# Smaller token tiles in the first mixture-of-experts layer of a two-layer perceiver kernel

## The chip, the cores and the metric

The kernel is one program on one core of a Trainium2 chip. The metric is the device time of one execution in microseconds (us). TensorE (PE) multiplies, VectorE (DVE), ScalarE (ACT) and GpSimd (POOL) do the element-wise work, and SyncE (SP) issues most of the transfers, which all run on the core's 16 DMA engines.

## The reference, cut to what matters

Two layers transform 512 tokens of 512 numbers. Each has a cross attention over 8192 context rows, a sequence mixer and a mixture of experts. The change concerns the experts of the first layer:

```
capacity = int(512 / 8 * 1.25) + 1            # 81
top1 = argmax(softmax(x @ wg));  rank = place of the token among those of its expert
valid = rank < capacity                        # tokens beyond the 81st get nothing
buf[expert * capacity + rank] = x              # 8 experts x 81 rows x 512
h = gelu(buf @ W1 + b1)                        # 512 -> 2048
y = h @ W2 + b2                                # 2048 -> 512
out = where(valid, y[slot], 0) * combine_w;  x = x + out
```

In the second layer each token goes to two of eight experts without a limit.

## The kernel before

The stages run one after the other, with a barrier between them: `ProjectContext` (keys and values of both layers from the context, 32 chunks of 512 rows), `CrossAttention`, `SelectiveScan`, `Experts` (layer 0), then attention, `DeltaRule` and `Experts` (layer 1). The same class does both expert layers; `self.two` is true in layer 1.

**Experts of layer 0.** A tile is the rows of one expert, so there are 8 tiles (`self.tiles`). Rows travel through two scratch tensors in HBM, `x_slots` and `y_slots`, in which tile `j` has the 128 rows `j * P` to `(j + 1) * P`. A token has row `e * 128 + rank`, or a spare row in tiles 8 to 11 if it is beyond capacity. Only rows 0 to 80 of a tile can be named by a token. POOL scatters the normalized rows into `x_slots` (L1562), and at the end gathers from `y_slots` (L1568). Tile 0 takes no such way in: `select_x` (L1581) builds it by a matmul with a 0/1 matrix. The last tile takes no such way out: its result is spread by a matmul (L1650).

**Weights.** Each tile needs 8 pieces of 1 MB of weights (4 of W1, 4 of W2), `moe_raw`, six buffers (`RAW`). Every fp32 operand is cut into a high and a low fp32r part: ACT makes the high part (L1656), DVE the low part (L1660), both of 128 x 2048 elements, three pieces ahead of PE (`AHEAD`), into four buffers (`CUT`). `product` (L93) then makes three matmuls of each pair. In all of them the token rows are the stationary operand and the 512 columns of the weights are the moving one, so a piece is 12 matmuls of 512 columns. For each of four blocks of 512 hidden numbers, `leave_hidden` copies the result (L1680), PE turns it (`turn_hidden`, four transposes, L1609), ACT applies gelu with the bias (L1691, four instructions of 128 x 128), and DVE makes the high and low parts (L1744, L1746). After the second W2 piece of a tile PE turns the next tile's rows (`turn_x`, L1588), and ACT and DVE cut them (L1671, L1728). DVE adds the output bias (L1783) and raises `y_done`.

**Order of the transfers.** SP works through one list in order (`loads_and_stores`, L1519). A piece `g` waits for the low part of piece `g - 6`. Ahead of pieces 6 and 7 of tile `j` stands the store of tile `j - 1`, which waits for its `y_done`; behind piece 0 of tile `j` stand the load of its rows and the load of its output bias (256 KB). So at each `y_done` SP sends, back to back, the store of the finished tile, pieces 6 and 7 of the tile that begins, piece 0 of the one after it, that tile's rows and bias, and then pieces 1 to 5 as buffers come free.

**Zeros.** In iteration 2 of `ProjectContext` SP stores zeros over all of `x_slots` (15 stores of 256 KB, L201) and over six tiles of `y_slots` (L203). The other tiles of `y_slots` get all their rows from the experts. Behind them in SP's list stand the store of the chunk's values (L226) and, in the next iteration, four stores of 512 KB of cut context (L172), on which `split_chunk` of ACT (L285) waits two iterations later (`parts_out`), and a store of the queries (L731).

Of the kernel before, what the change touches and what calls it, by code (L numbers as in the profile page):

```python
# [5 lines left out]
F32 = mybir.dt.float32  # L6
# [20 lines left out]
CAPACITY = int(TOK / EXPERTS * 1.25) + 1  # L27
FT = FF // P
# [71 lines left out]
class ProjectContext:  # L100
# [62 lines left out]
    def loads_and_stores(self, sp):  # L163
# [29 lines left out]
        for m in range(self.CHUNKS):  # L193
# [4 lines left out]
            if m == self.STORE_ZEROS:  # L198
                sp.wait_ge(*self.zeroed.at(1))
                for t in range(TILES1):  # L200
                    sp.dma_start(S["x_slots"][t * P:(t + 1) * P, :], self.nothing[:]).then_inc(*self.zeros_out.up())  # L201
                for tile in (EXPERTS - 1, *range(EXPERTS, EXPERTS + TT), TILES1 - 1):
                    sp.dma_start(S["y_slots"][tile * P:(tile + 1) * P, :], self.nothing[:]).then_inc(*self.zeros_out.up())  # L203
# [1086 lines left out]
class Experts:  # L1290
# [11 lines left out]
    def __init__(self, c, A, S, x, l, out=None):  # L1302
# [4 lines left out]
        self.choices = 2 if self.two else 1  # L1307

    def run(self):
        c, l = self.c, self.l  # L1310
        with ExitStack() as st:
# [22 lines left out]
            self.xg = c.sb(st, n + "xg", [P, 2, 2, KD, P], F32R)  # L1334
            self.h = c.sb(st, n + "h", [P, FF])
            self.ht = c.sb(st, n + "ht", [P, 2, FT, P], F32R)
            self.yrow = c.sb(st, n + "yrow", [P, 2, D])
            if not self.two:
                self.bias1 = c.sb(st, n + "bias1", [P, EXPERTS, FT])
                self.bias2 = c.sb(st, n + "bias2", [P, 2, D])  # L1340
                self.act_out = c.sb(st, n + "act_out", [P, 2, self.JB, P])
# [177 lines left out]
    def loads_and_stores(self, sp):  # L1519
        n, xs, ys = f"moe{self.l}_w", self.S["x_slots"], self.S["y_slots"]  # L1520

        def store(j):
            sp.wait_ge(*self.y_done.at(j + 1))
            sp.dma_start(ys[j * P:(j + 1) * P, :], self.yrow[:, j % 2, :]).then_inc(*self.y_out[j % 2].up())
# [3 lines left out]
        for j in range(self.tiles):  # L1528
# [3 lines left out]
            for w in range(self.pieces):  # L1532
# [4 lines left out]
                if w == (5 if j == 0 else 0):  # L1537
# [4 lines left out]
                    if j:  # L1542
                        sp.dma_start(self.xrow[:, j % 2, :], xs[j * P:(j + 1) * P, :]).then_inc(*self.xrow_in[j % 2].up())
# [30 lines left out]
    def on_pe(self, pe):  # L1574
        c, bank, ht, cut, JB = self.c, self.c.bank, self.ht, self.cut, self.JB

        def select_x():
            pe.wait_ge(*self.selected.at(TT))
            for k in range(KD):
                for t in range(TT):  # L1580
                    last = pe.matmul(bank[self.X_BANK][:, k * P:(k + 1) * P], self.norm.rows[:, t, k * P:(k + 1) * P], self.select[:, t, :], start=t == 0, stop=t == TT - 1)  # L1581
            last.then_inc(*self.x_turned.up())

        def turn_x(j):
            pe.wait_ge(*self.xrow_in[j % 2].at((j + 1) // 2))
            pe.wait_ge(*self.xg_low.at(j))
            for k in range(KD):
                last = pe.transpose(bank[self.X_BANK][:, k * P:(k + 1) * P], self.xrow[:, j % 2, k * P:(k + 1) * P], c.ident[:])  # L1588
# [8 lines left out]
        def out_of_hidden(g, db):  # L1597
            pe.wait_ge(*self.low.at(g + 1))
            for i in range(JB):
                f = db * JB + i  # L1600
                last = product(pe, bank[self.OUT_BANK], [ht[:, part, f, :] for part in range(2)], [cut[:, g % self.CUT, part, i, :] for part in range(2)], f == 0, f == FT - 1)
            last.then_inc(*self.used.up())

        def turn_hidden(j, fb):
# [3 lines left out]
            for i in range(JB):  # L1608
                last = pe.transpose(bank[self.TURN_BANK + fb % 2][:, i * P:(i + 1) * P], self.h[:, (fb * JB + i) * P:(fb * JB + i + 1) * P], c.ident[:])  # L1609
            last.then_inc(*self.h_turned.up())  # L1610

        def tile(j):
# [7 lines left out]
            for fb in range(FB):  # L1620
# [5 lines left out]
                else:  # L1626
                    into_hidden(j, g + fb, bank[fb])
# [21 lines left out]
        for t in range(TT):  # L1649
            pe.matmul(bank[t], self.spread_t[:, t, :], self.yrow[:, (self.tiles - 1) % 2, :], start=True, stop=True).then_inc(*self.last_made.up())  # L1650
# [11 lines left out]
    def on_act(self, act):  # L1662
        bank, JB, last_piece = self.c.bank, self.JB, self.tiles * self.pieces
# [5 lines left out]
        def x_high(j):  # L1669
            act.wait_ge(*self.x_turned.at(j + 1))  # L1670
            act.copy(self.xg[:, j % 2, 0], bank[self.X_BANK].rearrange("p (k n) -> p k n", k=KD)).then_inc(*self.xg_high.up())  # L1671

        def leave_hidden(j, fb):
# [4 lines left out]
            else:  # L1678
                act.wait_ge(*self.used.at(j * self.pieces + fb + 1))
                act.copy(part, bank[fb]).then_inc(*self.h_done.up())  # L1680

        def leave_turned(j, fb):
# [7 lines left out]
            for i in range(JB):  # L1690
                act.activation(self.act_out[:, fb % 2, i, :], b[:, i * P:(i + 1) * P], ACT.Gelu, bias=self.bias1[:, j, fb * JB + i:fb * JB + i + 1]).then_inc(*self.gelu.up())  # L1691
# [27 lines left out]
    def on_dve(self, dve):  # L1719
        bank, JB, last_piece = self.c.bank, self.JB, self.tiles * self.pieces  # L1720
# [5 lines left out]
        def x_low(j):  # L1726
            dve.wait_ge(*self.xg_high.at(j + 1))
            dve.tensor_tensor(self.xg[:, j % 2, 1], bank[self.X_BANK].rearrange("p (k n) -> p k n", k=KD), self.xg[:, j % 2, 0].bitcast(F32), ALU.subtract).then_inc(*self.xg_low.up())  # L1728
# [31 lines left out]
        for j in range(self.tiles):  # L1760
# [15 lines left out]
            if not self.two:  # L1776
# [6 lines left out]
                dve.tensor_tensor(self.yrow[:, j % 2, :], bank[self.OUT_BANK], self.bias2[:, j % 2, :], ALU.add).then_inc(*self.y_done.up())  # L1783
# [597 lines left out]
```

## Time and profile before

| | |
|---|---|
| Time, median of 3 runs | 3687.98 us (3680.82 to 3688.92) |
| Span of the profiled execution | 3690.2 us (no other time is given for it) |
| PE, DVE, ACT, POOL busy | 97%, 70%, 54%, 48% of the span |
| First expert layer | from about 1705 to 1932 us of the span |
| Mean DMA rate | 170 GB/s |

The span runs from the first to the last instruction. Busy time of an engine is a share of that; PE's is counted from modelled ends of pipelined matmuls, so 97% doesn't mean that 97% is work at full speed. The question for each stage is which engine, or which transfer, sets its pace.

### The profile page before, as it was taken

Reading aid. Unit: us, or ns where it says so; the run is one execution under the profiler, and the core shown is the slowest. Engines: PE = TensorE matmul, PEld = TensorE weight load, DVE = VectorE, ACT = ScalarE, POOL = GpSimd, SP = SyncE. Lnnn points to the kernel's source line nnn. Section 1 sums busy time; section 2 is a strip of 40 time slices with the busy share of each in tenths; the row PEclk is TensorE's granted clock in tenths of the full one; section 3 lists DMA queues with packets and bytes.
Section 4 is the critical chain, followed back from the end, with each engine's and each line's share of the span. In section 5 each row is a group of like instructions: output and inputs, shape, how many; then the busy total and the mean of one; then the engine's idle time right before and its main releaser. Section 6 shows DMA issues by size and latency. Waiting matters only on the chain. (4 is left out here: it accounts for less than half of the span.)

```text
span 3690.2 us, 46629 instructions
## 1 busy us (share of the span) xinstructions
PE 3575.8 (97%) x17916; PEld 2313.7 (63%) x17916; DVE 2570.7 (70%) x3497; ACT 1981.7 (54%) x2320; POOL 1781.2 (48%) x744
## 2 busy tenths in 40 slices
PE   8999999999999999988999999999999897999999
PEld 6788788654554555446876545555554476788887
DVE  3222344587787787557996877877876465899998
ACT  2122322466666666634973666666666421777776
POOL 2122222489889989700001889989988320100001
PEclk9999999999999999998998999999999998999999
DMA  7777776532332332046978433333331100999998
GB/s 274 252 246 228 244 236 202 178 92 69 91 92 71 88 92 73 18 173 224 362 296 237 108 91 72 89 92 77 83 92 31 52 1 20 366 376 368 379 377 302
DMA packets 249723, 628.46 MB, mean 170 GB/s; under 512 B 43632, under 2 KB 137872, under 8 KB 194976
## 3 DMA queue, kind: packets, MB, share of 16 engines
q1 hardware_dynamic: 210720, 552.08, 46.2%
q10 hardware_dynamic: 36864, 67.13, 4.9%
q0 software_dynamic: 1920, 6.29, 0.5%
q8 instruction: 143, 2.34, 0.3%
q14 instruction: 76, 0.62, 0.1%
HBM read 488.46 MB, written 136.87 MB: 169 GB/s over the span
## 5 line engine op out<-in xcount | busy, mean ns | idle before, releaser
L790 DVE TENSOR_REDUCE maxima<-psum 128x1 f32<-128x512 f32 x2048 | 1286.1, 683 | 344.2 <-PE psum L785 341.6
L961 POOL TENSOR_TENSOR exp_sums<-pt 128x1024 f32<-128x1024 f32 x342 | 816.8, 2389 | 296.0 <-PE psum L834 147.1
L785 PE MATMUL psum<-ks,first_q 96*128 96x512 f32 x2048 | 805.4, 434 | 4.8 <-DMA ks<-k_parts 0.6
L949 ACT ACTIVATE pt<-psum 128x1024 f32<-128x1024 f32 x704 | 717.6, 1026 | 142.7 <-PE psum L814 116.2
L964 POOL TENSOR_TENSOR exp_sums<-exp_sums,pt 128x1024 f32<-128x1024 f32 x310 | 737.4, 2379 | 44.4
L830 PE MATMUL psum<-pt,vs 128*32 128x512 f32 x4096 | 675.6, 600 | 7.1 <-issue 2.3
L785 PEld LDWEIGHTS psum<-ks,first_q 96*128 96x128 f32 x2048 | 386.9, 189 | 455.2 <-DVE maxima L790 318.1
L834 PE MATMUL psum<-exp_sums,constants 128*32 128x512 f32 x1408 | 671.4, 600 | 0.0
L814 PE MATMUL psum<-qs,ks 97*128 97x512 f32 x2048 | 656.2, 404 | 3.1 <-PEq L87 3.1
L1660 DVE TENSOR_TENSOR moe_cut<-moe_raw,moe_cut 128x2048 fp32r<-128x2048 f32 x244 | 556.9, 2290 | 55.9 <-ACT moe_cut L1656 48.6
L1656 ACT CAST moe_cut<-moe_raw 128x2048 fp32r<-128x2048 f32 x244 | 468.9, 1923 | 55.5 <-PE psum L97 47.0
L944 ACT ACTIVATE pt<-psum 128x512 f32<-128x512 f32 x320 | 191.2, 597 | 482.4 <-PE psum L814 480.1
L814 PEld LDWEIGHTS psum<-qs,ks 97*128 97x128 f32 x2048 | 389.5, 191 | 96.0 <-ACT pt L949 18.2
L372 POOL TENSOR_TENSOR cparts<-cx,cparts 128x2048 fp32r<-128x2048 f32 x32 | 147.8, 4620 | 521.5 <-ACT cparts L285 521.5
L830 PEld LDWEIGHTS psum<-pt,vs 128*32 128x32 f32 x4096 | 139.9, 109 | 342.4 <-issue 240.5
L1568 POOL DMA_INDIRECT ln_m_rows<-y_slots,row_of x8 | 13.2, 1653 | 667.2 <-DMA y_slots<-moe_yrow 665.4
L354 DVE SCALAR_TENSOR_TENSOR kparts<-psum,bk,kparts 128x512 fp32r<-128x512 f32 x128 | 96.1, 751 | 274.4 <-ACT kparts L311 274.4
L95 PE MATMUL psum<-moe_cut,moe_xg 128*128 128x512 f32 x608 | 241.6, 397 | 3.3 <-DVE moe_xg L1728 3.3
L97 PE MATMUL psum<-moe_cut,moe_xg 128*128 128x512 f32 x608 | 237.4, 390 | 0.0
L96 PE MATMUL psum<-moe_cut,moe_xg 128*128 128x512 f32 x608 | 236.6, 389 | 0.0
L95 PE MATMUL psum<-cparts,wk_high 128*128 128x512 f32 x512 | 205.7, 402 | 19.8 <-POOL cparts L372 16.8
L311 ACT ACTIVATE kparts<-psum,bk 128x512 fp32r<-128x512 f32 x128 | 88.1, 688 | 245.1 <-PE psum L97 227.3
(337 smaller groups left out, 4835.3 us busy)
## 6 DMA issues: line engine op xcount, KB each, us to landing
moe_raw<-in_moe_w SPq DMA_DIRECT2D x244, 1024.0 KB, 8.3
ks<-k_parts SPq DMA_DIRECT2D x384, 256.0 KB, 4.6
k_parts<-kparts ACTq DMA_DIRECT2D x256, 256.0 KB, 4.2
cx<-in_ctx SPq DMA_DIRECT2D x32, 1024.0 KB, 6.2
vs<-v_heads SPq DMA_DIRECT2D x32, 1024.0 KB, 5.3
v_heads<-vrow SPq DMA_DIRECT2D x25, 1024.0 KB, 5.1
late_context<-cparts SPq DMA_DIRECT2D x28, 512.0 KB, 11.7
late_parts<-late_context SPq DMA_DIRECT2D x28, 512.0 KB, 4.6
```

The source lines that it names most:

```text
L95: pe.matmul(out, lhs[0], rhs[0], start=start, stop=False)
L97: return pe.matmul(out, lhs[1], rhs[0], start=False, stop=stop)
L785: pe.matmul(self.c.bank[self.FIRST_BANK + k % 3], self.first_q[s][:, t * P:(t + 1) * P], self.ks[s][part][0:3 * DH, at:at + CHUNK], start= ...
L790: dve.tensor_reduce(self.maxima[:, h % 2, i % TT, i // TT:i // TT + 1], self.c.bank[self.FIRST_BANK + k % 3], X, ALU.max).then_inc(*self.f ...
L814: last = pe.matmul(bank[self.SECOND_BANK + 2 * (pair % 2) + j], ks[h % 2][part][:, at:at + P], qs[h % 2][:], start=True, stop=True)
L830: last = pe.matmul(bank[self.OUT_BANK][g * DH:(g + 1) * DH, :], vs[h % 2][:, tiles[i], :], pt[:, slot + i, :], start=b == 0 and r == 0, st ...
L834: last = pe.matmul(bank[self.OUT_BANK][3 * DH:4 * DH, :], c.ones[:, 0:DH], item, start=b == 0 and r == 0, stop=b == NB - 1 and r == min(se ...
L949: act.activation(self.pt[:, to:to + 2, :], self.c.psum[:, at:at + 2, :], ACT.Exp).then_inc(*self.exp.up())
L961: engine.tensor_tensor(to, self.pt[:, slot:slot + R, :], self.pt[:, slot + R:slot + 2 * R, :], ALU.add).then_inc(*signal.up())
L964: engine.tensor_tensor(to, to, self.pt[:, slot + (n + 1) * R:slot + (n + 2) * R, :], ALU.add).then_inc(*signal.up())
L1656: act.copy(self.cut[:, g % self.CUT, 0], self.raw[:, g % self.RAW]).then_inc(*self.high.up())
L1660: dve.tensor_tensor(self.cut[:, g % self.CUT, 1], self.raw[:, g % self.RAW], self.cut[:, g % self.CUT, 0].bitcast(F32), ALU.subtract).then ...
```

## The change

`ROWS0` is 82: the capacity of 81, made even. A tile of layer 0 is held in 82 rows in place of 128 (`self.held`); layer 1 keeps 128. In layer 0 this changes:

- the stationary operands have 82 columns, the moving ones still 512, and outputs lie in 82 partitions;
- the transposes take 82 rows and an 82 x 82 identity, `select_x` moves 82 columns;
- ACT and DVE instructions on `xg`, `ht` and `act_out` handle 328 or 82 columns in place of 512 or 128, those on `h` and `yrow` 82 partitions and still 512 columns;
- the load of a tile's rows and the store of a tile's result cover 82 rows of 2 KB (168 KB) in place of 128 (256 KB). The tile's place in HBM stays 128 rows apart. The bias load stays at 128 rows;
- `ProjectContext` gets seven more stores of zeros, over rows 82 to 127 of tiles 0 to 6 of `y_slots` (46 rows, 94 KB each), because no expert writes these any longer. They stand between the 15 stores to `x_slots` and the six to `y_slots`.

The cutting of the weights, the number of matmuls and the order of SP's list in the expert stage don't change.

```diff
+ROWS0 = CAPACITY + CAPACITY % 2
...
                 for t in range(TILES1):
                     sp.dma_start(S["x_slots"][t * P:(t + 1) * P, :], self.nothing[:]).then_inc(*self.zeros_out.up())
+                for tile in range(EXPERTS - 1):
+                    sp.dma_start(S["y_slots"][tile * P + ROWS0:(tile + 1) * P, :], self.nothing[ROWS0:P, :]).then_inc(*self.zeros_out.up())
                 for tile in (EXPERTS - 1, *range(EXPERTS, EXPERTS + TT), TILES1 - 1):
...
+        self.held = P if self.two else ROWS0
...
-            self.xg = c.sb(st, n + "xg", [P, 2, 2, KD, P], F32R)
+            self.xg = c.sb(st, n + "xg", [P, 2, 2, KD, self.held], F32R)
...
-            self.ht = c.sb(st, n + "ht", [P, 2, FT, P], F32R)
+            self.ht = c.sb(st, n + "ht", [P, 2, FT, self.held], F32R)
...
-                self.act_out = c.sb(st, n + "act_out", [P, 2, self.JB, P])
+                self.act_out = c.sb(st, n + "act_out", [P, 2, self.JB, self.held])
...
-            sp.dma_start(ys[j * P:(j + 1) * P, :], self.yrow[:, j % 2, :]).then_inc(*self.y_out[j % 2].up())
+            sp.dma_start(ys[j * P:j * P + self.held, :], self.yrow[0:self.held, j % 2, :]).then_inc(*self.y_out[j % 2].up())
...
-                        sp.dma_start(self.xrow[:, j % 2, :], xs[j * P:(j + 1) * P, :]).then_inc(*self.xrow_in[j % 2].up())
+                        sp.dma_start(self.xrow[0:self.held, j % 2, :], xs[j * P:j * P + self.held, :]).then_inc(*self.xrow_in[j % 2].up())
...
-                    last = pe.matmul(bank[self.X_BANK][:, k * P:(k + 1) * P], self.norm.rows[:, t, k * P:(k + 1) * P], self.select[:, t, :], start=t == 0, stop=t == TT - 1)
+                    last = pe.matmul(bank[self.X_BANK][:, k * P:k * P + R], self.norm.rows[:, t, k * P:(k + 1) * P], self.select[:, t, 0:R], start=t == 0, stop=t == TT - 1)
...
-                last = pe.transpose(bank[self.X_BANK][:, k * P:(k + 1) * P], self.xrow[:, j % 2, k * P:(k + 1) * P], c.ident[:])
+                last = pe.transpose(bank[self.X_BANK][:, k * P:k * P + R], self.xrow[0:R, j % 2, k * P:(k + 1) * P], c.ident[0:R, 0:R])
...
-                last = product(pe, bank[self.OUT_BANK], [ht[:, part, f, :] for part in range(2)], [cut[:, g % self.CUT, part, i, :] for part in range(2)], f == 0, f == FT - 1)
+                last = product(pe, bank[self.OUT_BANK][0:R, :], [ht[:, part, f, :] for part in range(2)], [cut[:, g % self.CUT, part, i, :] for part in range(2)], f == 0, f == FT - 1)
...
-                last = pe.transpose(bank[self.TURN_BANK + fb % 2][:, i * P:(i + 1) * P], self.h[:, (fb * JB + i) * P:(fb * JB + i + 1) * P], c.ident[:])
+                last = pe.transpose(bank[self.TURN_BANK + fb % 2][:, i * P:i * P + R], self.h[0:R, (fb * JB + i) * P:(fb * JB + i + 1) * P], c.ident[0:R, 0:R])
...
-                    into_hidden(j, g + fb, bank[fb])
+                    into_hidden(j, g + fb, bank[fb][0:R, :])
...
-            act.copy(self.xg[:, j % 2, 0], bank[self.X_BANK].rearrange("p (k n) -> p k n", k=KD)).then_inc(*self.xg_high.up())
+            act.copy(self.xg[:, j % 2, 0], bank[self.X_BANK].rearrange("p (k n) -> p k n", k=KD)[:, :, 0:R]).then_inc(*self.xg_high.up())
...
-                act.activation(self.act_out[:, fb % 2, i, :], b[:, i * P:(i + 1) * P], ACT.Gelu, bias=self.bias1[:, j, fb * JB + i:fb * JB + i + 1]).then_inc(*self.gelu.up())
+                act.activation(self.act_out[:, fb % 2, i, :], b[:, i * P:i * P + R], ACT.Gelu, bias=self.bias1[:, j, fb * JB + i:fb * JB + i + 1]).then_inc(*self.gelu.up())
...
-                dve.tensor_tensor(self.yrow[:, j % 2, :], bank[self.OUT_BANK], self.bias2[:, j % 2, :], ALU.add).then_inc(*self.y_done.up())
+                dve.tensor_tensor(self.yrow[0:R, j % 2, :], bank[self.OUT_BANK][0:R, :], self.bias2[0:R, j % 2, :], ALU.add).then_inc(*self.y_done.up())
```

The copy out of the hidden banks (L1680), the low part of the rows (L1728) and the spreading matmul of the last tile (L1650) are cut to `R` in the same way.

## Rows read from the trace of the kernel before

**Rows 1.** Busy time by stretch, all engines (stretch, us, engines, PEclk, DMA share, GB/s).

```profile
core 0: us, PE busy (x) PEld busy (x) DVE busy (x) ACT busy (x) POOL busy (x), PEclk, DMA share, GB/s
1761.00:1905.00 144.00, 144.00 (x696) 119.13 (x695) 140.12 (x114) 128.90 (x175) 0.00 (x0) 1.00 0.95 383
1767.00:1783.00 16.00, 16.00 (x80) 13.25 (x79) 15.90 (x14) 14.16 (x19) 0.00 (x0) 1.00 1.01 418
1784.00:1786.00 2.00, 2.00 (x11) 1.65 (x10) 2.00 (x3) 1.72 (x2) 0.00 (x0) 1.00 0.25 102
1725.10:1731.10 6.00, 5.85 (x32) 5.66 (x32) 4.63 (x17) 0.23 (x2) 2.08 (x1) 0.64 0.60 247
...
80.00:110.00 30.00, 30.00 (x119) 21.81 (x117) 8.90 (x13) 5.35 (x6) 4.52 (x1) 1.00 1.06 373
110.00:120.00 10.00, 10.00 (x44) 7.88 (x43) 3.85 (x6) 0.97 (x1) 0.00 (x0) 1.00 0.39 122
```

**Rows 2.** Groups by line and shape, 1704 to 1932 us (busy, mean ns, idle before).

```profile
L1660 DVE TENSOR_TENSOR moe_cut<-moe_raw,moe_cut 128x2048 fp32r<-128x2048 f32 x64 | 145.6, 2287 | 12.5 <-ACT moe_cut L1656 12.5
L1656 ACT CAST moe_cut<-moe_raw 128x2048 fp32r<-128x2048 f32 x64 | 124.2, 1944 | 8.4 <-PE psum L97 5.1 <-DMA moe_raw<-in_moe_w 3.2
...
L1691 ACT ACTIVATE moe_act_out<-psum,moe_bias 128x128 f32<-128x128 f32 x128 | 37.8, 408 | 0.0
...
L1609 PE MATMUL psum<-constants,moe_h 128*128 128x128 f32 x128 | 19.1, 272 | 0.0
```

**Rows 3.** Chain of waits, 1761 to 1905 us: who waited for whom, total, times, longest.

```profile
ACT moe_cut L1656 <- DMA moe_raw<-in_moe_w: 2.3, 3, 1.1
```

**Rows 4.** SP's queue in order of time (start, us, line, transfer, count).

```profile
1761.00 0.33 SPq L1524 DMA_DIRECT2D y_slots<-moe_yrow  x1
1761.37 1.41 SPq L1536 DMA_DIRECT2D moe_raw<-in_moe_w  x3
1762.82 0.60 SPq L1543 DMA_DIRECT2D moe_xrow<-x_slots  x1
...
1904.88 0.33 SPq L1524 DMA_DIRECT2D y_slots<-moe_yrow  x1
1905.25 0.92 SPq L1536 DMA_DIRECT2D moe_raw<-in_moe_w  x2
```

**Rows 5.** Store of a tile's result, 1704 to 1935 us: issue to landing.

```profile
DMA to landing us min/median/max: 2.1/2.2/3.1
```

**Rows 6.** PE in order of time about a group of transposes.

```profile
1810.70 0.39 PE L97 MATMUL psum<-moe_cut,moe_xg 128*128 128x512 f32 x1
...
1810.93 0.60 PE L1609 MATMUL psum<-constants,moe_h 128*128 128x128 f32 x4
...
1811.28 0.48 PE L95 MATMUL psum<-moe_cut,moe_xg 128*128 128x512 f32 x1
...
1811.60 0.40 PE L96 MATMUL psum<-moe_cut,moe_xg 128*128 128x512 f32 x1
```

**Rows 7.** End of the stage: the gathers (ns, first and last start), landing, and DVE.

```profile
L1568 POOL DMA_INDIRECT ln_m_rows<-y_slots,row_of x4: 949/1472/2186, 1907.3 to 1912.1; - x4
...
DMA to landing us min/median/max: 4.1/4.6/6.3
...
1921.09 2.73 DVE L1755 SCALAR_TENSOR_TENSOR x_rows<-ln_m_rows,small,x_rows 128x512 f32<-128x512 f32 x4
1925.92 0.69 DVE L1783 TENSOR_TENSOR moe_yrow<-psum,moe_bias 128x512 f32<-128x512 f32 x1 [2.10 <-PE psum L97]
```

**Rows 8.** About the stores of zeros: SP, ACT and DVE in order of time.

```profile
72.57 14.93 SPq L201 DMA_DIRECT2D x_slots<-nothing  x15
...
92.47 0.64 SPq L226 DMA_DIRECT2D v_heads<-vrow  x1
...
119.03 1.91 ACT L285 CAST cparts<-cx 128x2048 fp32r<-128x2048 f32 x1 [13.86 <-PE psum L97]
...
133.41 0.43 DVE L724 CAST qparts<-qf 128x512 fp32r<-128x512 f32 x1 [3.36 <-DMA q_parts<-qparts]
```

More of the change, by code:

```diff
@@ L1574, in on_pe @@
     def on_pe(self, pe):
-        c, bank, ht, cut, JB = self.c, self.c.bank, self.ht, self.cut, self.JB
+        c, bank, ht, cut, JB, R = self.c, self.c.bank, self.ht, self.cut, self.JB, self.held
         def select_x():
@@ L1649, in on_pe @@
         for t in range(TT):
-            pe.matmul(bank[t], self.spread_t[:, t, :], self.yrow[:, (self.tiles - 1) % 2, :], start=True, stop=True).then_inc(*self.last_made.up())
+            pe.matmul(bank[t], self.spread_t[0:R, t, :], self.yrow[0:R, (self.tiles - 1) % 2, :], start=True, stop=True).then_inc(*self.last_made.up())
     def high_part(self, act, g):
@@ L1662, in on_act @@
     def on_act(self, act):
-        bank, JB, last_piece = self.c.bank, self.JB, self.tiles * self.pieces
+        bank, JB, R, last_piece = self.c.bank, self.JB, self.held, self.tiles * self.pieces
         def high(g):
@@ L1679, in leave_hidden @@
                 act.wait_ge(*self.used.at(j * self.pieces + fb + 1))
-                act.copy(part, bank[fb]).then_inc(*self.h_done.up())
+                act.copy(part[0:R, :], bank[fb][0:R, :]).then_inc(*self.h_done.up())
         def leave_turned(j, fb):
@@ L1719, in on_dve @@
     def on_dve(self, dve):
-        bank, JB, last_piece = self.c.bank, self.JB, self.tiles * self.pieces
+        bank, JB, R, last_piece = self.c.bank, self.JB, self.held, self.tiles * self.pieces
         def low(g):
@@ L1727, in x_low @@
             dve.wait_ge(*self.xg_high.at(j + 1))
-            dve.tensor_tensor(self.xg[:, j % 2, 1], bank[self.X_BANK].rearrange("p (k n) -> p k n", k=KD), self.xg[:, j % 2, 0].bitcast(F32), ALU.subtract).then_inc(*self.xg_low.up())
+            dve.tensor_tensor(self.xg[:, j % 2, 1], bank[self.X_BANK].rearrange("p (k n) -> p k n", k=KD)[:, :, 0:R], self.xg[:, j % 2, 0].bitcast(F32), ALU.subtract).then_inc(*self.xg_low.up())
         def leave_hidden(j, fb):
```

## The prediction

> **What bounds the kernel now.** I read the busy time by stretch first, to find what sets the pace of the stage that changes. From 1761 to 1905 us, six tiles of the first expert layer, PE has no gap: 144.00 of 144.00 us, at the full granted clock [rows 1]. Between the first and the last store of a tile's result lie 143.88 us for six tiles, so a tile takes 23.98 us [rows 4]. DVE is busy 140.12 us of the 144, ACT 128.90, and the DMA engines 95%, so three others stand close behind PE. The groups by line say what they do: DVE's time is mostly the 64 low parts of the weights at 2287 ns, ACT's the 64 high parts at 1944 ns [rows 2]; neither depends on how many rows a tile has. The waits show that transfers are late three times, 2.3 us in all [rows 3], and those waits are ACT's, not PE's. So PE's stream is the bound, and behind it the transfers have little left: in a stretch with a full queue they run at 418 GB/s with a share of 1.01 [rows 1], which is 26.1 GB/s for each of 16 engines.
>
> **What the change does to PE.** The 96 matmuls of a tile move 512 columns as before, so they cost what they cost. What shrinks is the moving operand of 20 transposes a tile. Between the L97 before a group of four and the second matmul after it lie 0.90 us [rows 6]; an ordinary step takes 0.23 us, as from that L97 to the first transpose, and two of them lie in it, so four transposes cost 0.44 us, 0.11 us each. Bounds for one with 82 columns: nothing saved (if the load of its 128 columns of weights sets the step), or 46/128 of it, 0.04 us. That is 0 to 0.8 us a tile, 0 to 6 us for eight. `select_x`, 32 records in 5.85 us, lies on the path at the start, mostly at the low clock (0.64 [rows 1]); it gives 0 to 2.1 us by the same ratio. The first cut of the rows on ACT and DVE gives some 0.3 us. If nothing else moves, the change is worth 0 to 8 us; I would take 4.
>
> **ACT and DVE.** Gelu on 82 columns in place of 128 is shorter than 408 ns, and L1744 and L1746 handle 328 columns in place of 512. At most 46/128 of 16 x 0.41 us on ACT goes, 2.4 us a tile, and DVE loses at most 46/128 of its small work (about 23.35 us a tile less 8 x 2.29, so 5.1), 1.8 us. Both lie beside PE's stream. Their worth is nothing as long as PE has no gap.
>
> **The transfers.** A tile's rows and its result shrink from 262 KB to 168 KB each. Spread over all 16 engines that lowers the load of an engine from 573 to 562 KB a tile (8 pieces of 65.5 KB, the bias 16.4, and 2 x 10.5 in place of 2 x 16.4). But nothing in this trace shows a transfer of 82 rows of 2 KB, and 82 rows can't be dealt out evenly over 16: 128 is 16 x 8, 82 is 2 x 41. The two ends are 16 engines (5 or 6 rows each) and 2 engines (41 rows each); 128-row transfers run near 16 x 26.1 GB/s [rows 1], which fits equal shares and says nothing of 82. I take 2 engines: an equal deal is the simplest rule by which hardware could cut a copy without a remainder, and 2 is the largest number up to 16 that divides 82.
>
> The Trainium skill says so outright ("DMA: Bandwidth & Descriptors", section "Why a DMA increments its semaphore by 16 and not by 1"): a copy issued from SP uses the largest number of engines up to 16 that divides the slowest dimension of both sides, always the lowest-numbered ones. By it both 82-row and 46-row copies run on the same 2 engines; no row here tests it.
>
> **Price of 2 engines in the expert stage.** Each of the two engines then carries 8 x 65.5 + 16.4 + 2 x 84.0 = 708 KB a tile. At 26.1 GB/s that is 27.1 us, more than PE's 23.98. A weight piece has landed only when its slowest engine is done, so from then on the tile takes 27.1 us. The slack ahead of PE takes up part. I therefore count the queue of these two engines through to the end, from the first store of a result, at 1761.00 [rows 4]. SP has been standing there, and the queue runs empty while it does, as the share of 0.25 just about the next store, at 1784 to 1786 us, shows [rows 1]. In front of the last piece stand 50 pieces (14 to 63), 7 stores of results, 6 loads of rows, 6 of the bias: 3275 + 588 + 504 + 98 = 4465 KB, 171.1 us. A store of 256 KB into an empty queue lands 2.2 us after its issue [rows 5], of which 0.6 us is moving 16.4 KB per engine, so 1.6 us is fixed. The last piece lands at 1761.0 + 1.6 + 171.1 = 1933.7. Behind it come ACT 1.94, DVE 2.29 [rows 2] and 12 matmuls at 0.23, 2.8 us: PE is done at 1940.7, against 1925.9 before (start of L1783 [rows 7]): **+14.8 us**. The queue stays full in between: at each `y_done` SP hands it a store, three pieces, the next rows and the bias, and then five pieces as buffers come free, 27.1 us of work for a tile.
>
> What is late next is the gather. It starts when the store of tile 6 has landed, before at 1907.3; now that store has pieces 62 and 63 behind it, 5.0 us, so it lands at 1928.7. The last of four gathers is issued 4.8 us later and lands at most 6.3 us after that [rows 7], 1939.8; DVE's last add-back of 0.7 us ends at 1940.5. That is just when PE ends, so I add 0.3. Stage: **+15 us**. PE's 0 to 8 us are not seen then, since the transfers set the end.
>
> **Price in the first stage.** The seven new stores of zeros (46 rows, 94 KB) have the same problem: 46 is 2 x 23. They give two engines 47 KB each seven times, 330 KB, 12.6 us. Spread evenly they would be 659 KB, 1.6 us. They stand behind the 15 stores to `x_slots`, which SP issues at 1.0 us each, the pace of full queues [rows 8]. From 80 to 110 us the DMA share is 1.06, and in the next 10 us 0.39 [rows 1], so only about 6 us of those 12.6 find free room. Late then are the store of values (92.47), the four stores of cut context, on which ACT's cut at 119.03 depends, and the store of queries, on which DVE already waited 3.36 us at 133.41 [rows 8]. Bounds: 0 (ACT's K work and PE have slack of several us) and 12.6 (all passed on). I take 4, since the last of those waits has no slack.
>
> **Sum.** 15 + 4 = +19 us: the profiled execution, whose span of 3690.2 is the only time given for it and lies 2.2 above the median, would show 3709; on the median of 3688, **3707 us**.
>
> **The rivals.**
>
> *Even spreading.* If an 82-row copy uses all 16 engines, the load per engine falls, the zeros are hidden, and PE's savings are all that is left: 3688 - 4 = 3684, range 3680 to 3688. This is the case that ends faster, or unchanged. The mechanism decides by the number of engines: with n of them a loaded engine carries 541 + 336/n KB, and 23.98 us at 26.1 GB/s is 626 KB, so with 4 or more PE remains the bound. For it speaks only that nothing in the trace contradicts it. Chance 0.12.
>
> *Two engines, but absorbed.* The weights are issued up to six pieces ahead, 6 x 2.5 = 15 us. If the queue's lead over PE at 1761 covers more than my count, or an engine alone runs faster than 26.1 GB/s when the other 14 rest, the stage loses under 5 us: 3688 to 3694. Against it: the count runs to the last piece, and the lead is in it, since the last piece is now issued at 1906 and used only at 1923 or so. The rate would have to rise to 28.5 GB/s to take the 14.8 away. Chance 0.07.
>
> *Two engines, and slower than counted.* Copies of 2 KB rows cost an engine more than pieces of 8 KB a partition, and rows and results both are of that kind. At 20 GB/s for those 13 transfers (84 KB, 4.2 us in place of 3.2) the stage loses 13 us more, and the zeros up to 8 more: 3721 to 3728. The 15 stores of zeros, of the same rows, fill the engines at 373 GB/s for 80 to 110 us [rows 1], 0.9 of the rate I used, so a little of this is likely. Chance 0.11.
>
> *Forecast as summed*: 0.70, its own range 3697 to 3720.
>
> **How the numbers follow.** The likeliest case gives 3707. Eight in ten: below 3689 lies the even spreading, 0.11 or so, above 3725 the worst of the slower case, 0.07; hence 3689 to 3725. A change of this kernel can be told from none at about 0.2%, 7.4 us. Faster by more: half of the even case at best, 0.04. Within: the rest of that case and most of the absorbed one, with a little of the forecast's low end, 0.13. Slower: 0.83.
>
> **What the changed profile would show.** The store of a result should land 5 us or more after its issue where it took 2.2, even into an empty queue (3.2 us of moving in place of 0.6). The distance from one such store to the next should grow from 23.98 to about 27 us, with PE idle before L1588 and L95, and ACT's L1656 waiting for `moe_raw`. The DMA share of 1761 to 1905 should fall below 0.95 though the stage is bound by transfers, as 14 engines rest. SP should be stuck for some 12 us more at the stores of zeros, and PE should show gaps, or a late start, between 105 and 140 us. The gelu of 82 columns should be under 408 ns and change nothing. The prediction is wrong if the result's store still lands in 2.2 us: then the copy is spread, and the time is PE's.

## The result

The changed kernel takes 3725.95 us (median of 4 runs, 3724.44 to 3727.28), the kernel before, on the same chip, 3686.81 (4 runs, 3680.82 to 3688.92): a ratio of 1.0106, 95% interval 1.0091 to 1.012. The change costs 39 us. The forecast was 3707, with 3725 as the upper end of its range: right in direction, and some 19 us too small. The profiled execution has a span of 3725.3 us, 35.1 more than before's 3690.2.

The lines of `Scratch` and of the expert stage stand four lines lower in the new file: before's L1524, L1543, L1568, L1588, L1656, L1660, L1691 and L1783 are L1528, L1547, L1572, L1592, L1660, L1664, L1695 and L1787 here.

**SP's queue** of the changed kernel, in order of time (start, us, line, transfer, count), first about the zeros and then in the expert stage:

```profile
93.26 12.29 SPq L206 DMA_DIRECT2D y_slots<-nothing  x6
105.60 1.13 SPq L229 DMA_DIRECT2D v_heads<-vrow  x1
...
1712.56 0.35 SPq L1362 DMA_DIRECT2D wr<-in_moe_router  x1
...
1769.26 0.26 SPq L1528 DMA_DIRECT2D y_slots<-moe_yrow  x1
...
1857.38 0.26 SPq L1528 DMA_DIRECT2D y_slots<-moe_yrow  x1
...
1886.30 0.26 SPq L1528 DMA_DIRECT2D y_slots<-moe_yrow  x1
...
1948.11 0.26 SPq L1528 DMA_DIRECT2D y_slots<-moe_yrow  x1
...
1976.35 0.33 SPq L679 DMA_DIRECT2D wq<-in_wq  x1
```

L1528 is the store of a tile's result, as L1524 was [rows 4]. From the first to the last there are now 1948.11 - 1769.26 = 178.85 us for six tiles, **29.81 us a tile** where it was 23.98 and the forecast said 27.1. The next stage's first load stands at 1976.35; before it stood at 1933.52. From the router's load at the top (1712.56; before 1705.21) the expert stage takes 263.8 us in place of 228.3, which is 35.5 more. And the stage begins 7.35 us later, most of which comes from the zeros: SP is stuck for 12.29 us in six of them, and the store of values that stood at 92.47 [rows 8] now stands at 105.60.

**Busy time by stretch** of the changed kernel (columns as in [rows 1]):

```profile
1769.26:1948.11 178.85, 153.58 (x697) 99.66 (x696) 134.58 (x114) 125.14 (x174) 0.00 (x0) 0.92 0.80 302
1873.00:1876.00 3.00, 0.29 (x3) 0.16 (x3) 2.97 (x4) 0.75 (x1) 0.00 (x0) 1.00 0.99 314
1876.00:1880.00 4.00, 4.00 (x14) 2.54 (x14) 0.88 (x2) 1.51 (x2) 0.00 (x0) 0.57 1.03 424
1824.00:1826.00 2.00, 2.00 (x11) 1.26 (x10) 1.79 (x2) 1.41 (x2) 0.00 (x0) 1.00 0.13 53
```

PE had no gap in these six tiles [rows 1]; now it is busy 153.58 of 178.85 us. The last line shows why. From 1824 to 1826 us ACT is still working through pieces as they land, yet the DMA share is 0.13 and 53 GB/s move. Two of 16 engines are 0.125, and twice 26.1 GB/s are 52. So 14 engines have nothing to do, while two carry the tail of every weight piece. The packets of the transfers say the same of all six tiles: exactly two engines are at work in 5.5 us of a tile, and one or none in 0.3 us. So the two loaded engines hardly ever rest. The share of the whole stretch fell from 0.95 to 0.80 in a stage that is now bound by its transfers.

**The chain of waits** of the changed kernel, 1769 to 1948 us (who waited for whom: total, times, longest):

```profile
DVE moe_cut L1664 <- ACT moe_cut L1660: 35.8, 29, 3.5
ACT moe_cut L1660 <- DMA moe_raw<-in_moe_w: 25.7, 22, 2.4
...
PE psum L1592 <- DMA moe_xrow<-x_slots: 20.3, 5, 5.3
...
PE psum L1592 <- issue: 4.6, 1, 4.6
```

ACT waited 2.3 us in all for weight pieces [rows 3]; now it waits 25.7. PE itself waits 20.3 us in five waits at L1592, the transposes of the next tile's rows, the first of the two places that the forecast gave it. A sixth wait of 4.6 us, for which the profile names no releaser, stands at the same line. Together these are 24.9 of PE's 25.3 idle us. At the second place, the first matmul of a product, it never waits: the pieces come late for ACT, but still in time for PE, and what stops PE is the load of the next rows, which stands in the same queue behind the store and three pieces. One of the six, **PE in order of time**:

```profile
1872.74 0.40 PE L98 MATMUL psum<-moe_cut,moe_ht 128*82 128x512 f32 x1
1875.84 0.51 PE L1592 MATMUL psum<-constants,moe_xrow 82*128 82x82 f32 x4 [2.71 <-DMA moe_xrow<-x_slots]
1876.14 0.44 PE L96 MATMUL psum<-moe_cut,moe_ht 128*82 128x512 f32 x1
1876.42 0.48 PE L97 MATMUL psum<-moe_cut,moe_ht 128*82 128x512 f32 x1
1876.69 0.63 PE L98 MATMUL psum<-moe_cut,moe_ht 128*82 128x512 f32 x1
1877.12 0.63 PE L96 MATMUL psum<-moe_cut,moe_ht 128*82 128x512 f32 x1
```

Behind a wait of 2.71 us the steps between matmuls are 0.43 us in place of 0.23, and the granted clock of 1876 to 1880 is 0.57, mostly the lower level of 1.2 GHz. That makes PE slow for some 3 us just after it stood idle. It costs little here, since the two loaded engines stay at work meanwhile and set the pace.

**The store of a result.** The profile gives no landing for the stores of 82 rows, but their packets can be followed. The last of the 82 ends 5.4 to 7.0 us after the issue, 5.5 in the median; of the 128 before, 1.7 to 2.6 us, 1.7 in the median. In the store of 1797.88 all 82 packets take 84 ns, and they fill 3.41 us: that is 41 of them one behind the other, on each of two engines. The gather behind the last store, in the changed kernel:

```profile
L1572 POOL DMA_INDIRECT ln_m_rows<-y_slots,row_of x4: 950/1438/2561, 1954.2 to 1958.9; - x4
```

The first gather waits for the last store and comes 6.1 us after its issue (1948.11), where before it came 2.4 us after [rows 4, 7]. Even so it starts 14.6 us and the last one 9.9 us before the addition of the last product's bias (L1787), which starts at 1968.8 and waits for PE alone, 1.5 us. So the gather is not late.

### The profile page after: what moved, and what is told of

Same layout as the page of the kernel before. It is cut to its first block and busy times, and to the rows that moved or that the text cites. A ratio compares the mean times of both kernels' runs of the same rounds, so it can differ in the third digit from the quotient of the medians.

```text
span 3725.3 us, 46636 instructions
## 1 busy us (share of the span) xinstructions
PE 3578.3 (96%) x17916; PEld 2282.1 (61%) x17916; DVE 2561.5 (69%) x3497; ACT 1976.1 (53%) x2320; POOL 1781.2 (48%) x744
## 5 line engine op out<-in xcount | busy, mean ns | idle before, releaser
L1664 DVE TENSOR_TENSOR moe_cut<-moe_raw,moe_cut 128x2048 fp32r<-128x2048 f32 x244 | 557.6, 2291 | 93.0 <-ACT moe_cut L1660 87.0
L1660 ACT CAST moe_cut<-moe_raw 128x2048 fp32r<-128x2048 f32 x244 | 467.3, 1916 | 79.5 <-PE psum L98 44.8
L1572 POOL DMA_INDIRECT ln_m_rows<-y_slots,row_of x8 | 14.1, 1766 | 708.1 <-DMA y_slots<-moe_yrow 706.3
L96 PE MATMUL psum<-moe_cut,moe_xg 128*128 128x512 f32 (+1 forms) x608 | 241.9, 398 | 3.2 <-DVE moe_xg L1732 3.2
L98 PE MATMUL psum<-moe_cut,moe_xg 128*128 128x512 f32 (+1 forms) x608 | 238.0, 391 | 0.0
L97 PE MATMUL psum<-moe_cut,moe_xg 128*128 128x512 f32 (+1 forms) x608 | 237.5, 391 | 0.0
```

Source lines behind the costliest of these rows:

```text
L96: pe.matmul(out, lhs[0], rhs[0], start=start, stop=False)
L98: return pe.matmul(out, lhs[1], rhs[0], start=False, stop=stop)
L1660: act.copy(self.cut[:, g % self.CUT, 0], self.raw[:, g % self.RAW]).then_inc(*self.high.up())
L1664: dve.tensor_tensor(self.cut[:, g % self.CUT, 1], self.raw[:, g % self.RAW], self.cut[:, g % self.CUT, 0].bitcast(F32), ALU.subtract).then ...
```

## The experiments

Ten kernels, in an order that narrows the question: is it the number of rows in a copy, what do the zeros cost, which copy costs what, how does it go with the number of engines, and can the 82 rows be kept at no cost. "Tile" below is the distance between the first and the last store of a result, by six; "stage" runs from the router's load to the next stage's first load. Each ratio is against the kernel before on the same chip. The products and transposes have 84, 96 and 92 columns in e1, e2 and e8, 128 in e4_zeros46, and 82 in the others.

| kernel | rows in the stage's copies | tile, us | stage, us | median, us | before, us | ratio (95%) |
|---|---|---|---|---|---|---|
| before | 128 | 23.98 | 228.3 | | | |
| after | 82 | 29.81 | 263.8 | 3725.95 | 3686.81 | 1.0106 (1.0091 to 1.012) |
| e1_rows84 | 84 | 23.49 | 226.1 | 3680.45 | 3687.08 | 0.9981 (0.9972 to 0.999) |
| e2_rows96 | 96 | 23.75 | 225.8 | 3680.39 | 3687.08 | 0.9982 (0.9973 to 0.9991) |
| e3_dma128 | 128, products 82 | 23.46 | 225.8 | 3681.29 | 3687.08 | 0.9985 (0.9976 to 0.9994) |
| e4_zeros46 | before, with the zeros | 23.98 | 228.3 | 3693.42 | 3687.08 | 1.0019 (1.001 to 1.0029) |
| e5_zeros48 | 82, zeros 48 | 29.76 | 263.4 | 3717.14 | 3687.02 | 1.0084 (1.0071 to 1.0098) |
| e6_x82 | load 82, store 128 | 26.51 | 242.7 | 3698.88 | 3687.02 | 1.004 (1.0026 to 1.0054) |
| e7_y82 | load 128, store 82 | 24.97 | 236.2 | 3690.15 | 3687.02 | 1.001 (1.0001 to 1.0019) |
| e8_rows92 | 92 | 26.27 | 242.6 | 3696.75 | 3687.02 | 1.0028 (1.0017 to 1.0039) |
| e9_bias82 | bias 82, the rest 128 | 26.69 | 242.8 | 3698.49 | 3685.83 | 1.003 (1.0018 to 1.0042) |
| e10_split82 | 80 + 2, zeros 48 | 23.46 | 226.1 | 3681.13 | 3685.83 | 0.9985 (0.9976 to 0.9994) |

### The number of rows in a copy: e1, e2, e3

e1_rows84 against the changed kernel (84 is 14 x 6; the zeros are then 44 rows, 11 x 4):

```diff
-ROWS0 = CAPACITY + CAPACITY % 2
+ROWS0 = 84
```

> The changed kernel with 84 rows to a tile in place of 82: two rows more in every load, store, matmul and copy. Two-engine theory (a copy is dealt out in equal parts, over the largest number of engines up to 16 that divides its rows): 84 is 14 x 6 and the zeros' 44 rows are 11 x 4, so no engine gets much more than the others; the tile is back at PE's pace of 24.0 us or a little below, the first stage at its old length, the time 3680 to 3690 us. Rival (any copy of fewer than 128 rows is slow, or 82-column operands are): 84 is no better than 82, about 3725 us, a tile takes about 30 us.

e2_rows96 (96 is 16 x 6; the zeros are then 32 rows):

```diff
-ROWS0 = CAPACITY + CAPACITY % 2
+ROWS0 = 96
```

> The changed kernel with 96 rows to a tile: 96 is 16 x 6 and the 32 rows of zeros 16 x 2. Two-engine theory: all 16 engines share each copy, tile at PE's pace, 3680 to 3690 us, the same as with 84 rows within a microsecond or two. Rival (fewer rows are slow in themselves): between the kernels before and after, 3700 to 3715 us.

e3_dma128 computes with 82 rows, but copies 128 in both directions and stores no zeros; POOL clears `yrow` once in their place:

```diff
-                for tile in range(EXPERTS - 1):
-                    sp.dma_start(S["y_slots"][tile * P + ROWS0:(tile + 1) * P, :], self.nothing[ROWS0:P, :])...
...
-            sp.dma_start(ys[j * P:j * P + self.held, :], self.yrow[0:self.held, j % 2, :])...
+            sp.dma_start(ys[j * P:(j + 1) * P, :], self.yrow[:, j % 2, :])...
...
-                        sp.dma_start(self.xrow[0:self.held, j % 2, :], xs[j * P:j * P + self.held, :])...
+                        sp.dma_start(self.xrow[:, j % 2, :], xs[j * P:(j + 1) * P, :])...
...
+            pool.memset(self.yrow[:], 0.0).then_inc(*self.cleared.up())
...
+                if j == 0:
+                    dve.wait_ge(*self.cleared.at(1))
```

> The changed kernel with the two transfers of a tile back at 128 rows and without the seven stores of zeros; all of PE, ACT and DVE works on 82 rows as in the changed kernel. If the transfers are the whole loss, the time is at or below that of before, and the tile shows what the smaller compute is worth: 23.2 to 24.0 us for 23.98, 3679 to 3688 us. If the 82-row compute has a part in the loss, a tile stays above 24.5 us.

Two rows more take the whole loss away and turn it into a gain: 3680.45 where 82 rows gave 3725.95. e1, e2 and e3 agree within 1 us, though their copies hold 84, 96 and 128 rows. The first and the last store of a result in e1_rows84 (the row of the `moe_yrow` tile: ns min/median/max, first and last start):

```profile
L1528 SPq DMA_DIRECT2D y_slots<-moe_yrow x7: 340/340/341, 1757.6 to 1898.5; - x7
```

140.9 us for six tiles, against 178.85 with 82 rows. So the cause is how a copy of 82 rows is dealt out, and not its bytes, the shapes of the products or the zeros as such. This is also what the rule that the prediction cites (the Trainium skill, "DMA: Bandwidth & Descriptors", section "Why a DMA increments its semaphore by 16 and not by 1") makes of these sizes: 14 engines for 84 rows, 16 for 96 and 128, 2 for 82. The trace agrees with the 2 (share 0.13 at 53 GB/s), the times with the rest. A rival rule, the largest power of two that divides the rows, would put 84 rows on 4 engines, as it does the 92 of e8 below; but e8 has a tile of 26.27 us and e1 one of 23.49.

In e3_dma128 PE again has no gap, and the four transposes can be read (PE in order of time):

```profile
1811.55 0.39 PE L98 MATMUL psum<-moe_cut,moe_xg 128*82 128x512 f32 x1
1811.78 0.45 PE L1613 MATMUL psum<-constants,moe_h 82*128 82x82 f32 x4
1812.02 0.44 PE L96 MATMUL psum<-moe_cut,moe_xg 128*82 128x512 f32 x1
1812.30 0.40 PE L97 MATMUL psum<-moe_cut,moe_xg 128*82 128x512 f32 x1
```

From the L98 before them to the second matmul behind them 0.75 us, where it was 0.90 [rows 6]: with two steps of 0.23 in it, four transposes cost 0.29 us, 0.07 each, for 0.11. Twenty of them should save 0.75 us a tile; the tile fell by 0.52 (23.98 to 23.46). The median step between the other matmuls went from 0.227 to 0.230 us, which over 96 of them takes some 0.3 back.

### The zeros: e4, e5

e4_zeros46 is the kernel before with the seven stores of zeros and nothing else of the change:

```diff
+                for tile in range(EXPERTS - 1):
+                    sp.dma_start(S["y_slots"][tile * P + 82:(tile + 1) * P, :], self.nothing[82:P, :])...
```

> The kernel before with nothing but the seven stores of 46 rows of zeros added. Two-engine theory: the first stage is some 7 us longer as in the changed kernel, and the rest is unchanged, 3692 to 3697 us. Rival (the zeros are hidden and the later start of the expert stage has another cause): 3685 to 3689 us.

e5_zeros48 is the changed kernel with zeros over rows 80 to 127 (48 is 16 x 3; the results overwrite rows 80 and 81 later):

```diff
-                    sp.dma_start(S["y_slots"][tile * P + ROWS0:(tile + 1) * P, :], self.nothing[ROWS0:P, :])...
+                    sp.dma_start(S["y_slots"][tile * P + 80:(tile + 1) * P, :], self.nothing[80:P, :])...
```

> The changed kernel (82 rows) with the seven stores of zeros over rows 80 to 127, 48 rows, 16 x 3, in place of 46. Two-engine theory: the first stage is back at its old length, the expert stage keeps its whole loss: about 7 us less than the changed kernel, 3717 to 3721 us, a tile still 29.8 us. Rival (the late start also costs the expert stage, or the 2 engines don't explain the zeros): no change, 3724 to 3728 us.

e4 costs 0.19%, 0.10 to 0.29%, 6 to 7 us. e5 gives 8.8 us back of the changed kernel's 39.1, across two chips (3717.14 for 3725.95), and the expert stage is as slow as ever (29.76 us a tile), so the two losses are separate; 6.3 and 30.1 us, each against its own kernel before, add up to 39.1 within the intervals. SP in e4_zeros46, in order of time:

```profile
92.54 11.96 SPq L205 DMA_DIRECT2D y_slots<-nothing  x6
104.55 1.28 SPq L228 DMA_DIRECT2D v_heads<-vrow  x1
...
1710.51 0.34 SPq L1360 DMA_DIRECT2D wr<-in_moe_router  x1
```

The 12 us at the zeros are the 12.6 that the prediction counted for two engines. What they hold up is seen in the changed kernel's chain of waits, 90 to 140 us:

```profile
DVE vrow L369 <- DMA v_heads<-vrow: 9.8, 1, 9.8
...
PE psum L96 <- DVE vrow L369: 4.6, 1, 4.6
```

The store of values is 13 us late, DVE waits 9.8 us before it can write `vrow` again, and PE 4.6 us for DVE, its only wait from 90 to 140 us. Right behind that wait PE has no gap, but the granted clock is at its lower level (busy time by stretch of the changed kernel):

```profile
118.00:122.00 4.00, 4.00 (x10) 3.13 (x11) 2.29 (x4) 0.00 (x0) 0.00 (x0) 0.50 1.04 315
```

There the matmuls start every 0.43 us in place of 0.23, nine times, which adds some 1.8 us. Together that is 6.4, and SP's stores of values show it later on; kernel before, changed kernel and e4:

```profile
193.68 0.38 SPq L226 DMA_DIRECT2D v_heads<-vrow  x1
...
200.52 0.39 SPq L229 DMA_DIRECT2D v_heads<-vrow  x1
...
199.42 0.39 SPq L228 DMA_DIRECT2D v_heads<-vrow  x1
```

Less what already lay between the kernels ahead of the zeros (0.12 us more, and 0.70 less, at the store of 66.24), the zeros cost 6.7 us in the changed kernel and 6.4 in e4. The start of the expert stage, 7.35 and 5.3 us later, is a poorer measure: in the kernels without the 46-row zeros it lies anywhere from 1700.7 to 1705.8, before included.

### Which copy: e6, e7

Both ask whether the load of rows and the store of the result cost the same. e6_x82 is e3_dma128 with the load back at 82 rows:

```diff
-                        sp.dma_start(self.xrow[:, j % 2, :], xs[j * P:(j + 1) * P, :])...
+                        sp.dma_start(self.xrow[0:self.held, j % 2, :], xs[j * P:j * P + self.held, :])...
```

> As e3 (all transfers of 128 rows, no extra zeros), but the load of a tile's rows covers 82. Load of the two engines by my 26.1 GB/s: 8 x 65.5 + 16.4 + 16.4 + 84 = 641 KB, 24.6 us a tile, so hardly over PE's 23.5: 3682 to 3686 us. If a 2 KB row costs such an engine more than at full rate (about 0.12 us in place of 0.08, as the tile of 29.8 us in the changed kernel asks): 20.2 + 0.7 + 1.3 + 4.9, 26.5 to 27 us a tile, 3695 to 3705 us. PE also waits ahead of the turning of the rows (L1592).

e7_y82 is the changed kernel with the load at 128 rows and the zeros at 48, so that only the store has 82:

```diff
-                    sp.dma_start(S["y_slots"][tile * P + ROWS0:(tile + 1) * P, :], self.nothing[ROWS0:P, :])...
+                    sp.dma_start(S["y_slots"][tile * P + 80:(tile + 1) * P, :], self.nothing[80:P, :])...
...
-                        sp.dma_start(self.xrow[0:self.held, j % 2, :], xs[j * P:j * P + self.held, :])...
+                        sp.dma_start(self.xrow[:, j % 2, :], xs[j * P:(j + 1) * P, :])...
```

> The changed kernel with the load of a tile's rows back at 128 and the zeros at 48 rows, but the store of a result at 82 rows. By 26.1 GB/s the same 24.6 us a tile and 3682 to 3686 us; by slow 2 KB rows 25.5 to 26.5 us a tile and 3690 to 3700 us. If load and store cost alike, e6 and e7 agree; the sum of their losses against e3 should be no more than the loss of e5, since each alone uses up part of the same slack.

They don't cost the same. The load alone makes the tile 26.51 us and the kernel 3698.88; the store alone makes it 24.97 and 3690.15, between the two values that its expectation gave for a tile. From here the tile of a loaded engine can be priced with the packets in the trace. A piece's packets of 8 KB take 0.314 us each where nothing slows them (26.1 GB/s), 8 to an engine and piece, 64 a tile: 20.1 us. The bias and the copy left at 128 rows have 8 packets of 2 KB each, at 0.084 us: 0.67 us for each of the two. What is left in e6 is 26.51 - 20.10 - 1.34 = 5.07 us for 41 rows of the load, **0.124 us a row** (16.5 GB/s). In e7 it is 24.97 - 21.44 = 3.53 us for 41 rows of the store, **0.086 us a row** (24 GB/s). Both together give 20.10 + 0.67 + 5.07 + 3.53 = 29.4, and 29.8 was measured. The packets themselves agree: in e6_x82, whose load has 82 of them, 88 of the 2 KB packets of a tile took 100 ns or more, 130 in the mean; in e7_y82 six did. In the changed kernel it is 84, at 143 ns, so a row of the load is dearer still when both copies have 82 rows. The prediction had 3.2 us for each and 20.7 for the rest.

The stage shows it within one tile of e6_x82 (busy time by stretch):

```profile
1797.00:1798.00 1.00, 1.00 (x6) 0.62 (x5) 1.00 (x1) 1.00 (x2) 0.00 (x0) 1.00 0.98 250
1800.00:1801.00 1.00, 0.00 (x0) 0.00 (x0) 1.00 (x1) 0.00 (x0) 0.00 (x0) 1.00 1.02 328
1804.00:1805.00 1.00, 1.00 (x4) 0.51 (x2) 0.07 (x1) 0.00 (x0) 0.00 (x0) 0.50 0.99 410
1811.00:1812.00 1.00, 1.00 (x6) 0.61 (x5) 1.00 (x1) 0.88 (x1) 0.00 (x0) 1.00 0.14 57
```

While the rows are being loaded all engines count as busy, and yet 250 to 328 GB/s move where 410 move a little later. The two engines' load slows the other 14 too. They have the time for it: at 1811 they rest, and the two go on at 57 GB/s.

### Four engines: e8

92 rows are 4 x 23, and the zeros are 36 rows, 12 x 3 or 4 x 9:

```diff
-ROWS0 = CAPACITY + CAPACITY % 2
+ROWS0 = 92
```

> The changed kernel with 92 rows: 92 is 4 x 23, so by the theory of equal parts each row transfer runs on 4 engines; the 36 rows of zeros run on 12. Load of a busy engine 541 + 2 x 47.1 = 635 KB, 24.3 us a tile at 26.1 GB/s, 25.5 with 2 KB rows at 0.12 us: 3683 to 3697 us, between 84 or 96 rows (3680) and 82 (3726). Rival (only 2 engines are slow, or any even share is good): 3680 as with 84.

Four engines don't get out of it: 3696.75, 1.0028 (1.0017 to 1.0039), slower than before. The tile by the prices of e6 and e7 is 20.10 + 0.67 + 23 x 0.21 = 25.6 us; measured are 26.27, so 0.7 us are not accounted for. With all rows at 26.1 GB/s it would be 24.3, hardly above PE's 23.98. Where the other engines rest, the trace shows the four:

```profile
1812.00:1815.00 3.00, 3.00 (x15) 2.03 (x14) 3.00 (x3) 2.91 (x3) 0.00 (x0) 1.00 0.28 115
```

Four of 16 are 0.25, and four times 26.1 GB/s are 104.

### Is it the direction: e9

A load of rows comes from a tensor that the kernel wrote itself, the bias from an input. If the source makes the load dear, the bias is cheap at 82 rows; if the direction does, both cost the same. e9_bias82 against e3_dma128:

```diff
-                        sp.dma_start(self.bias2[:, j % 2, :], self.A["moe0_b2"][j * P:(j + 1) * P, :])...
+                        sp.dma_start(self.bias2[0:self.held, j % 2, :], self.A["moe0_b2"][j * P:j * P + self.held, :])...
```

> As e3, but the load of a tile's output bias, which comes from an input and not from a scratch tensor, covers 82 rows; rows and results move in 128. It stands right behind the load of the rows. In e6 a load of 82 rows from x_slots made the tile 26.5 us, in e7 a store of 82 rows 25.0. If a load of 2 KB rows into 82 partitions is dear in itself, wherever it comes from: 26.0 to 26.5 us a tile and 3692 to 3700 us (PE doesn't wait for the bias as it does for the rows, so perhaps a little less than e6). If the scratch tensor is what makes it dear: 25.0 us a tile as with the store, about 3690 us.

26.69 us a tile, where the rows at 82 gave 26.51, and a little above the 26.0 to 26.5 that were expected. The source is of no matter: what is dear is a load of 82 rows into SBUF. PE doesn't wait at the rows here, but in five waits for the low parts of the weights (L1664), 8.4 us in all: whichever load is slow, what stands behind it in the queue comes late. The durations of the 2 KB packets, from the first to the last store of a result, show slow ones with other counts of rows too (ns: mean, quartiles and the 90% mark):

```
kernel        mean    25%  50%  75%  90%
before        85.1     84   84   84   85
e3 (128)      85.6     84   84   84   87
e7 (store 82) 87.5     84   84   84   84
e9 (bias 82)  95.4     84   84   92  131
e6 (load 82)  96.9     84   84  101  136
after        101.1     84   84  107  138
e8 (92)      108.0     84   84  125  144
e10 (80+2)   113.8     84  109  135  154
e2 (96)      113.4     84  107  133  158
e1 (84)      118.9     84  115  141  162
```

Every kernel whose loads have fewer than 128 rows has packets of 130 to 160 ns, also those at which the copy is spread over many engines. With five or six rows to an engine it no longer decides.

### 82 rows, spread: e10

If the count of engines is the cause, 82 rows cost nothing once they are cut into 80 (16 x 5) and 2. e10_split82 is the changed kernel with both copies in two parts and the zeros at 48:

```diff
+        self.shares = ((0, P),) if self.two else ((0, 80), (80, ROWS0))
...
-            sp.dma_start(ys[j * P:j * P + self.held, :], self.yrow[0:self.held, j % 2, :])...
+            for a, b in self.shares:
+                sp.dma_start(ys[j * P + a:j * P + b, :], self.yrow[a:b, j % 2, :])...
...
-                        sp.dma_start(self.xrow[0:self.held, j % 2, :], xs[j * P:j * P + self.held, :])...
+                        for a, b in self.shares:
+                            sp.dma_start(self.xrow[a:b, j % 2, :], xs[j * P + a:j * P + b, :])...
...
-            pe.wait_ge(*self.xrow_in[j % 2].at((j + 1) // 2))
+            pe.wait_ge(*self.xrow_in[j % 2].at(len(self.shares) * ((j + 1) // 2)))
```

> The changed kernel at 82 rows, with each load of rows and each store of a result issued as two copies, of 80 rows (16 x 5) and of 2, and the zeros at 48 rows. The bytes are the same as in the changed kernel, only the cuts are different. Two-engine theory: one row more on each of two engines is nothing, so the whole loss goes: tile 23.5 us, 3678 to 3684 us, as with 84 rows. Rival (82-row data are slow for another reason, or more copies cost SP time that matters): over 3690 us.

3681.13, 0.9985 (0.9976 to 0.9994), with 14 copies more than the changed kernel has. PE has no gap in its six tiles (busy time by stretch):

```profile
1759.88:1900.62 140.74, 140.74 (x695) 93.84 (x694) 133.07 (x114) 124.36 (x174) 0.00 (x0) 1.00 0.98 382
```

The same rows and the same products as in the changed kernel, and 44.8 us less across two chips. That shows the cause from the other side: the dealing out, of the rows and of the zeros, and nothing else of the change, made it slower.

## Why the prediction was right in direction and wrong in size

**That a copy of 82 rows runs on two engines: right.** The share of 0.13 at 53 GB/s and the 41 packets in a row show it, and e1, e2 and e10 take the loss away in three ways. The sign that the prediction named for it came too: the store is done over 5 us after its issue.

**"At 26.1 GB/s that is 27.1 us": the term that was mis-sized.** It priced rows of 2 KB like pieces of 8 KB a partition. The store is nearly so (0.086 us a row, 24 GB/s); the load isn't (0.124 us, 16.5 GB/s). 29.8 us a tile in place of 27.1 makes 6 x 2.7 = 16.3 us of the missing 20. The rival "two engines, and slower than counted" named this and gave it 0.11; it took 20 GB/s for both, 4.2 us each where 5.1 and 3.5 were measured, and up to 8 more from the zeros. Its 3721 to 3728 holds the result. The prediction had a row that spoke for it, 373 GB/s for the stores of zeros [rows 1], and priced nothing by it.

**The end of the stage: 3.6 us short.** The forecast let the last tile run from the last store to DVE's add-back in 17.1 us, as what the queue still had to bring and 7 us behind it. It took 1968.8 - 1948.11 = 20.7 us, near the 21.0 of before (1925.92 - 1904.88 [rows 4, 7]): the forecast let PE wait for the last weight piece, but in the trace it waits for the last tile's rows, and behind them it runs at its own pace, without a gap from the last store to L1787. 16.3 and 3.6 are the 19.8 us between +14.8 and the +34.6 that lie between the first store and L1787 (199.5 us for 164.9). Another 0.9 us lies ahead of the first store; together 35.5.

**The gather late next: wrong, but of little weight (0.3 us).** The last gather is issued 9.9 us before L1787 starts.

**The zeros, +4: 6.7 us.** The 12.6 us on two engines were right (12.29). The wait named as the critical one, for the store of queries, wasn't it: the store of values was, on which DVE waited 9.8 us and PE 4.6, with 4 us at the lower clock behind it, which the forecast had no term for. e4 alone gives 6.3 us (3.7 to 10.7).

**PE's 0 to 8 us: right.** A transpose fell from 0.11 to 0.07 us, and the stage from 228.3 to 225.8 or 226.1 once the transfers are out of the way (e1, e2, e3), where the forecast took 4 us. In the changed kernel none of it is seen, as forecast. ACT's gelu went from 408 to 339 ns and changed nothing.

**"With 4 or more engines PE remains the bound": wrong**, as far as e8 shows it: with 92 rows on 4 engines a tile takes 26.27 us. For 82 rows the prices of e6 and e7 give an estimate of 20.10 + 0.67 + 20.5 x 0.21 = 25.1, also above PE's 23.98. Which number of engines would just do wasn't tried between 4 and 14.

**Sum.** 7.35 + 35.5 = 42.8 us, but the span is only 35.1 longer. (The medians are 39.1 apart: the profiled execution of before was long for its kernel. A time lies 1.8 us above its span, so that one would be 3692, by this estimate 5 above its median.) The missing 7.7 us are in what follows the expert stage, which no step of the prediction spoke of. They hid part of the shortfall: without them the forecast would have been too small by some 28 us. From the next stage's first load to the end it takes 1756.7 us in the kernel before and in e4_zeros46, and 1749.0 in the changed kernel, 1749.0 to 1749.8 in e1, e2, e3 and e5 to e9, 1751.9 in e10. So of the 6 us by which e1 to e3 beat the kernel before, only 2.5 lie in the expert stage. Part of the difference is at the start of that next stage, where the clock differs. Kernel before:

```profile
1933.50:1943.50 10.00, 6.87 (x20) 4.79 (x21) 2.65 (x10) 3.83 (x6) 0.00 (x0) 0.54 0.88 341
```

Changed kernel:

```profile
1976.30:1986.30 10.00, 6.92 (x24) 4.86 (x25) 2.65 (x10) 3.84 (x6) 0.00 (x0) 0.69 0.88 333
```

The same work runs at a granted clock of 0.69 for 0.54 (that is, with less time at 1.2 GHz), and another 3.4 us are missing from the linear-attention stage that follows (214.0 to 210.6 us). What moves them was only looked at in the traces; no run tells it, and it stays open. Every kernel with 82 to 96 rows in its products has it, whatever it copies (e3 copies 128), and e4, with 128, doesn't.

What also stays open is why a load of fewer than 128 rows takes 0.124 us a row. e9 rules out the source tensor; nothing here separates the number of partitions written from where in SBUF they lie.

## What to carry to other kernels

Fewer bytes in a copy can cost more time: with 36% fewer bytes in 14 copies, each of them on two engines, a tile took 29.8 us whose transfers had fitted into 24. Ahead of a change to a tile's rows, find the largest number up to 16 that divides them, and price the busiest engine, not the sum over all; 84 or 96 rows, or 80 + 2, were worth 45 us here against 82. And price the busiest engine with the row size and the direction that it will have, and look for what stands behind the slow copies in the same queue: here the pieces of weights and the next tile's rows behind a result, and a store of values behind the zeros.

## What the hardware showed that was not expected

- A load into SBUF of 82 rows of 2 KB cost 0.124 us a row on its engine, a store of the same rows 0.086, the 128-row copies 0.084 (e6, e7, and the packets of before). With 84 and 96 rows a quarter of the 2 KB packets took 133 ns or more as well, so it isn't the two engines' doing.
- While such a load runs, packets of other copies are slower: a tenth of the 8 KB packets took 428 ns or more in the changed kernel and 455 in e6_x82, where before 320 was the 90% mark; all 16 engines count as busy at 250 to 330 GB/s.
- A PE wait of 2.7 us was followed, 1 us later, by some 3 us at 1.2 GHz, with DVE and the transfers running on; behind the wait of 4.6 us at the zeros the clock was at 0.50 from 118 to 122 us, and that one the kernel paid for.
